# Two feed-forward stages of a fused model: the three widths of the elastic one are added before a transposed down-projection in column strips, and each group's up-projection is issued ahead of the last group's down-projection

## The chip, the cores and the metric

One core of a Trainium2 chip. The time is the device time of one execution of the whole program, in microseconds (us); several runs are taken and the median is compared.

## What is computed

The reference is a small vision and text model: patch embedding, three attention layers and two feed-forward layers (FFN), on 16 samples of 144 slots (141 tokens and 3 of padding), so 2304 rows of 192 channels, all in float32. The change touches the two FFNs alone.

```python
def _mlp_branch(xp, w1, b1, w2, b2, keep_ch):
    C = xp.shape[-1]
    cmask = (jnp.arange(C) < keep_ch).astype(xp.dtype)
    h = jax.nn.gelu(xp * cmask @ w1 + b1, approximate=False)
    return (h @ w2 + b2) * cmask
...
# L0 FFN: first half of the batch wide, second half elastic
m_large = _mlp_branch(nl2, w_fc1, b_fc1, w_fc2, b_fc2, C)
m_small = sum((gumbel_weights[i] * _mlp_branch(ns2, w_fc1, b_fc1, w_fc2, b_fc2, C // ALPHA[i]) for i in range(3)))
...
# L1 FFN
h = jax.nn.gelu(jnp.einsum('td,hd->th', xt, in_weight) + in_bias, approximate=False)
out = jnp.einsum('th,ho->to', h, out_weight)
```

`ALPHA` is 1, 2, 3, so the elastic half of the L0 FFN evaluates widths of 192, 96 and 64 channels: each width needs its own gelu of 768 hidden units, and its own part of the down-projection reaches only the first 192, 96 or 64 output channels.

## The kernel before, in words

The 2304 rows are 18 tiles of 128 (`TILES`), and an FFN works in groups of 3 tiles (`GT_` = 384 columns of the transposed activations `XT`). The 768 hidden units are 6 blocks of 128 (`HM`), counted by `m`. `feed_forward` (L1198) is called three times: "wide" for groups 0 to 2 and "elastic" for groups 3 to 5 of the L0 FFN, "last" for the 6 groups of the L1 FFN. Each call is one block in which every engine has its own program, and engines meet by semaphores.

TensorE, per group: the up-projection of all six `m` into PSUM banks 0 to 5 (L1214), then a wait for the gelus of this very group (`s_gl`), then the down-projection of the three tiles (L1247) into banks 6 and 7 by turns. In the up-projection, 192 input channels are 128 and 64: the matmul of 128 rows fills the array, and two of 64 rows stand in its upper and lower half (`tile_position` (0, 0) and (64, 0)).
In the down-projection the hidden activations are the weights of the array (128 x 128) and the rows of `w2` move: 6 `m` for each tile, and in the elastic call 6 times three, with 192, 96 and 64 moving columns and three copies of `w2` (`m_w2a`, `m_w2b`, `m_w2c`) that GpSimd has scaled by the three gumbel weights ahead of the stage (`scale_mlp`, L1185). All three widths add up in one PSUM bank.

ScalarE evaluates the gelus (L1260), VectorE adds the PSUM bank, the saved `XN`, the bias row and `H` in three steps (`finish_m`, L1287), or in one step in the last FFN (`finish_l`, L1739). ScalarE and VectorE run loops over the groups. The buffer `hid` of the gelus is single: the gelus of the next group start only when TensorE issues its up-projection, which is behind the down-projection of the group before. The last FFN stores its output group by group.

Ahead of the L0 FFN, and behind both, stand stages that are not changed: `residual_norm` with its transposes (L492 to L501), and after the L0 FFN products of expert weights (L1319) beside the next norm.

Of the kernel before, what the change touches and what calls it, by code (L numbers as in the profile page):

```python
# [20 lines left out]
ALU = mybir.AluOpType  # L21
ACT = mybir.ActivationFunctionType
AX = mybir.AxisListType

P = 128
C = 192
# [31 lines left out]
def ds(a, n):  # L58
    return bass.ds(a, n)

def fusion_kernel(nc: bass.Bass, d: dict, out: bass.AP):
    with ExitStack() as ctx:
# [3 lines left out]
        def sem(name):  # L67
            return ctx.enter_context(nc.semaphore(name))
# [1077 lines left out]
        def lsb(stack, name, shape):  # L1146
            return stack.enter_context(nc.sbuf_tensor(name, shape, F32))
# [14 lines left out]
        m_w2a, m_w2b, m_w2c = (lsb(mlp, f"m_w2{x}", [P, HM, n]) for x, n in (("a", C), ("b", 96), ("c", 64)))  # L1162
        s_wm = sem("elastic_mlp_weights")

        def load_up(sp, dst, w, s):

# [18 lines left out]
        def scale_mlp(pool):  # L1185

            pool.wait_ge(w_ffn, UP_W + 16)
            for k, (w, n) in enumerate(((m_w2a, C), (m_w2b, 96), (m_w2c, 64))):
                nc.gpsimd.tensor_scalar(w[:, :, :], m_w2[:, :, 0:n], vecs[:, V_GUM + k:V_GUM + k + 1], None, ALU.mult
                                        ).then_inc(s_wm, 1)  # L1190

        residual_norm(XN, add_to_xn, False, False, (V_N2L, V_N2S), {"sync": load_late, "gpsimd_after": scale_mlp},
                      twin=True)

        GT_ = 3 * P

        def feed_forward(tag, w1, w2s, hid, ready, b1, groups, k_rows, finish, store=None):  # L1198

            nv = len(k_rows)
            units = nv * HM
            g0, g1 = groups
            (s_up, s_gl, s_dn, s_fn, s_x, s_store) = phase_sem([
                f"{tag}_hidden", f"{tag}_gelu", f"{tag}_down", f"{tag}_finished", f"{tag}_partial", f"{tag}_stored"])
            with nc.Block() as block:  # L1206
                @block.tensor
                def _(pe):
                    for s_w, n_w in ready:
                        pe.wait_ge(s_w, n_w)  # L1210
                    def up(g, u, m, c, lo, n, first, last):

                        cols = slice((g + g0) * GT_, (g + g0 + 1) * GT_)
                        return nc.tensor.matmul(bank[u % 6][:, 0:GT_], w1[lo:lo + n, c, m * P:(m + 1) * P],  # L1214
                                                XT[lo:lo + n, c, cols], start=first, stop=last, tile_position=(lo, 0))

                    def up_pair(g, m):

                        for x in range(2):
                            pe.wait_ge(s_gl, g * units + m + x + 1)  # L1220
                            up(g, m + x, m + x, 0, 0, P, True, False)
                        for x in range(2):
                            up(g, m + x, m + x, 1, x * C1, C1, False, True).then_inc(s_up, 1)

                    def up_variants(g, m):

                        u = m * nv
                        pe.wait_ge(s_gl, g * units + u + nv)
                        up(g, u, m, 0, 0, P, True, False)
                        up(g, u + 1, m, 0, 0, k_rows[1], True, True).then_inc(s_up, 1)  # L1230
                        up(g, u, m, 1, C1, C1, False, True).then_inc(s_up, 1)
                        up(g, u + 2, m, 0, 0, k_rows[2], True, True).then_inc(s_up, 1)

                    for g in range(g1 - g0):
                        if nv == 1:
# [5 lines left out]
                        pe.wait_ge(s_gl, (g + 1) * units + 6)  # L1241
                        for j in range(3):
                            pe.wait_ge(s_fn, g * 3 + (1 if j < 2 else 2))
                            for m in range(HM):
                                for v, w in enumerate(w2s):
                                    n = w.shape[2]
                                    mm = nc.tensor.matmul(bank[6 + j % 2][:, 0:n], hid[:, m * nv + v, j * P:(j + 1) * P],  # L1247
                                                          w[:, m, :], start=(m == 0 and v == 0),
                                                          stop=(m == HM - 1), skip_group_check=True)
                            mm.then_inc(s_dn, 1)  # L1250

                @block.scalar
                def _(act):
                    act.sem_inc(s_gl, 6)  # L1254
                    with act.Fori(0, g1 - g0) as g:  # L1255
                        for m in range(HM):
                            for x, v in enumerate((0,) if nv == 1 else (1, 0, 2)):
                                u = m * nv + v
                                act.wait_ge(s_up, g * units + m * nv + x + 1)
                                nc.scalar.activation(hid[:, u, :], bank[u % 6][:, 0:GT_], ACT.Gelu,  # L1260
                                                     bias=vecs[:, b1 + m:b1 + m + 1]).then_inc(s_gl, 1)

                @block.vector
                def _(dve):
                    dve.sem_inc(s_fn, 1)
                    with dve.Fori(0, g1 - g0) as g:
                        for j in range(3):
                            dve.wait_ge(s_dn, g * 3 + j + 1)
                            finish(dve, (g + g0) * 3 + j, g * 3 + j, bank[6 + j % 2][:, 0:C], s_x, s_fn)

                if store:
                    @block.sync
                    def _(sp):
                        with sp.Fori(0, g1 - g0) as g:
                            sp.wait_ge(s_fn, g * 3 + 4)
                            sp.dma_start(out.rearrange("(t p) n -> p t n", p=P)[:, ds((g + g0) * 3, 3), :],
                                         H[:, ds((g + g0) * 3, 3), :]).then_inc(s_store, 16)
                        sp.wait_ge(s_store, 16 * (g1 - g0))

        with ExitStack() as ph:  # L1280
            def psb(name, shape, dt=F32):
                return ph.enter_context(nc.sbuf_tensor(name, shape, dt))

            hid = psb("m_hid", [P, 3 * HM, GT_])
            part = psb("m_part", [P, C])

            def finish_m(row):  # L1287
                def finish(dve, tile, count, psum, s_x, s_fn):

                    h = H[:, ds(tile, 1), :].rearrange("p t n -> p (t n)")  # L1290
                    x = XN[:, ds(tile, 1), :].rearrange("p t n -> p (t n)")
                    nc.vector.tensor_tensor(part[:, :], psum, x, ALU.add).then_inc(s_x, 1)  # L1292
                    dve.wait_ge(s_x, count * 3 + 1)
                    nc.vector.tensor_tensor(part[:, :], part[:, :], rows[:, row, :], ALU.add).then_inc(s_x, 1)
                    dve.wait_ge(s_x, count * 3 + 2)
                    nc.vector.tensor_tensor(h, part[:, :], h, ALU.add).then_inc(s_x, 1)
                    dve.wait_ge(s_x, count * 3 + 3)
                    dve.sem_inc(s_fn, 1)
                return finish

            feed_forward("wide", m_w1, (m_w2,), hid, ((w_ffn, UP_W + 16),), V_B1, (0, 3), (C,), finish_m(B2L))
            feed_forward("elastic", m_w1, (m_w2a, m_w2b, m_w2c), hid, ((s_wm, 3),), V_B1, (3, 6), (C, 96, 64),
                         finish_m(B2S))

        end_phase()
        mlp.close()
# [426 lines left out]
        with ExitStack() as ph:  # L1733
            def psb(name, shape, dt=F32):
                return ph.enter_context(nc.sbuf_tensor(name, shape, dt))

            hid = psb("l_hid", [P, HM, GT_])

            def finish_l(dve, tile, count, psum, s_x, s_fn):  # L1739
                h = H[:, ds(tile, 1), :].rearrange("p t n -> p (t n)")  # L1740
                nc.vector.tensor_tensor(h, psum, h, ALU.add).then_inc(s_fn, 1)  # L1741

            feed_forward("last", g_w1, (g_w2,), hid, ((w_last, UP_W + 16),), V_FB, (0, 6), (C,), finish_l, store=True)
        end_phase()

# [93 lines left out]
```

## Time and profile before

| | us |
|---|---|
| median of 3 runs | 1338.97 |
| the three runs | 1335.55, 1338.97, 1340.47 |
| the profiled execution | 1340.07 |
| its span in the trace | 1338.3 |
| TensorE busy | 1199.4 |
| VectorE / ScalarE / GpSimd busy | 711.5 / 769.5 / 349.3 |
| L0 FFN, first matmul to last write of `H` | 448.5 to 584.6 |
| L1 FFN, first matmul to the end of the trace | 1247.3 to 1338.3 |

A count of matmuls in a row is a count of passes, and the busy time of a group of matmuls is the time in which any of them runs, so that of passes which overlap it is smaller than their number times the mean.

### The profile page before, as it was taken

The numbers are of one execution on the slowest core, as the hardware profiler recorded it, in microseconds if no ns is written. First come the engines' busy times: TensorE is split into PE (matmuls) and PEld (weight loads), VectorE is DVE, ScalarE is ACT, GpSimd is POOL, SyncE is SP. The second block draws the span as 40 slices with busy tenths as digits, with TensorE's granted clock in tenths as the row PEclk, the third lists the DMA queues.
The fourth block names the chain that finished last, engine by engine and source line by source line (L and its number), as shares of the span: only waits on it lengthen the run. The fifth ranks groups of instructions, "written<-read, shape, count | busy, mean of one in ns | idle before, by whom it ended". The sixth has DMA issues, their size and how long they took to land. (4 is left out here: it accounts for less than half of the span.)

```text
span 1338.3 us, 34162 instructions
## 1 busy us (share of the span) xinstructions
PE 1199.4 (90%) x13220; PEld 972.4 (73%) x13220; DVE 711.5 (53%) x2290; ACT 769.5 (57%) x3346; POOL 349.3 (26%) x477
## 2 busy tenths in 40 slices
PE   6789976999997789996899999999999999995898
PEld 5479944777774456653788888988888888983465
DVE  7344465666666110023666667666666667666100
ACT  2155525677773533302877777777777777773432
POOL 2100023333332000002334433444334433441000
PEclk9789966999996799976999999999999999996799
DMA  7000000000006200001000000000000000000000
GB/s 234 20 1 1 2 1 1 1 2 2 2 2 140 44 1 1 0 1 41 2 2 2 3 2 2 2 3 2 2 2 2 2 2 3 2 2 1 9 19 27
DMA packets 34734, 19.85 MB, mean 15 GB/s; under 512 B 24592, under 2 KB 32016, under 8 KB 34576
## 3 DMA queue, kind: packets, MB, share of 16 engines
q1 hardware_dynamic: 34432, 17.20, 4.8%
q8 instruction: 106, 1.74, 0.5%
q10 hardware_dynamic: 144, 0.49, 0.1%
q14 instruction: 52, 0.43, 0.1%
HBM read 15.12 MB, written 1.77 MB: 13 GB/s over the span
## 5 line engine op out<-in xcount | busy, mean ns | idle before, releaser
L1692 POOL TENSOR_TENSOR e_W<-e_W,e_RS 128x384 f32<-128x384 f32 x256 | 203.8, 827 | 349.6 <-DVE e_RS L1620 349.6
L1563 ACT ACTIVATE e_W<-banks,e_MX 128x128 f32<-128x128 f32 x768 | 268.9, 389 | 18.3 <-DVE e_MX L1608 18.2
L1563 ACT ACTIVATION_READ_ACCUMULATOR e_W<-banks,e_MX 128x1 f32 x768 | 176.1, 229 | 0.0
L1557 ACT COPY e_PT<-banks 128x512 f32<-128x512 f32 x128 | 69.0, 588 | 105.0 <-PE banks L1468 105.0
L1420 PE MATMUL banks<-XT,e_wqk 128*128 128x141 f32 x768 | 112.2, 297 | 11.9 <-DVE e_GU L1662 8.4
L469 POOL TENSOR_TENSOR rstd<-veps,nhalf 128x6 f32<-128x6 f32 x15 | 20.6, 1373 | 365.8 <-DVE veps L435 365.8
L1420 PEld LDWEIGHTS banks<-XT,e_wqk 128*128 128x128 f32 x768 | 98.5, 194 | 14.3 <-issue 11.6
L1468 PE MATMUL banks<-ident,e_W 128*128 128x128 f32 x768 | 105.5, 273 | 2.7 <-POOL e_W L1692 1.6
L1432 PE MATMUL banks<-e_wv,XT 128*128 128x192 f32 (+1 forms) x512 | 100.2, 339 | 0.3 <-ACT e_K L1552 0.2
L1468 PEld LDWEIGHTS banks<-ident,e_W 128*128 128x128 f32 x768 | 90.3, 141 | 6.2 <-POOL e_W L1692 1.9
L1608 DVE TENSOR_REDUCE e_MX<-banks 128x3 f32<-128x384 f32 x128 | 65.4, 553 | 42.8 <-PE banks L1456 42.8
L1117 POOL TENSOR_TENSOR f_W<-f_W,f_RS 128x423 f32<-128x423 f32 x64 | 56.3, 892 | 118.8 <-DVE f_RST L1101 110.9
L1260 ACT ACTIVATE m_hid<-banks,vecs 128x384 f32<-128x384 f32 x72 | 38.8, 577 | 77.7 <-PE banks L1214 77.7
L1432 PEld LDWEIGHTS banks<-e_wv,XT 128*128 128x128 f32 (+1 forms) x512 | 75.7, 168 | 6.1 <-ACT e_K L1552 0.6
L1484 PE MATMUL banks<-e_PT,e_V 128*32 128x128 f32 x1536 | 68.7, 277 | 9.9 <-DVE e_PTT L1628 9.9
L1214 PE MATMUL banks<-XT,m_w 128*128 128x384 f32 (+1 forms) x216 | 65.7, 538 | 8.0 <-ACTq L1254 8.0
L989 ACT ACTIVATE f_W<-banks,f_MX 128x141 f32<-128x141 f32 x192 | 70.2, 394 | 2.0 <-DVE f_MX L1036 1.4
L1292 DVE TENSOR_TENSOR m_part<-banks,XN 128x192 f32<-128x192 f32 x18 | 6.4, 358 | 120.6 <-PE banks L1247 120.6
L1620 DVE RECIPROCAL e_RS<-e_SM 128x3 f32<-128x3 f32 (+1 forms) x192 | 33.9, 176 | 63.6 <-ACT e_W L1563 63.4
L1484 PEld LDWEIGHTS banks<-e_PT,e_V 128*32 128x32 f32 x1536 | 51.6, 109 | 21.1 <-DVE e_PTT L1628 16.7
L1456 PE MATMUL banks<-e_K,e_Q 32*128 32x128 f32 x1536 | 63.2, 288 | 0.0
L880 PE MATMUL banks<-ident,f_W 128*70 128x128 f32 (+1 forms) x384 | 52.5, 277 | 9.3 <-DVE f_PT L1057 7.8
(245 smaller groups left out, 2743.2 us busy)
## 6 DMA issues: line engine op xcount, KB each, us to landing
xp<-in_patches_dram SPq DMA_DIRECT2D x4, 768.0 KB, 8.2
H<-in_h_dram SPq DMA_DIRECT2D x1, 1728.0 KB, 10.3
out_dram<-H SPq DMA_DIRECT2D x6, 288.0 KB, 2.3
e_g<-in_e_gu_dram SPq DMA_DIRECT2D x1, 1536.0 KB, 8.3
e_o<-in_e_o_dram SPq DMA_DIRECT2D x4, 192.0 KB, 5.9
e_wqk<-in_e_qk_dram SPq DMA_DIRECT2D x8, 96.0 KB, 2.6
e_wqk<-in_e_qk_dram SPq DMA_DIRECT2D x24, 32.0 KB, 2.3
e_wv<-in_e_v_dram SPq DMA_DIRECT2D x4, 192.0 KB, 2.6
```

What stands on the lines that cost most here:

```text
L989: ex = nc.scalar.activation(W[n % 2][:, t, :], bank[i][:, x * SEQ:(x + 1) * SEQ], ACT.Exp, bias=MX[:, t:t + 1], accum_out=SM[n % 2][:, t:t ...
L1117: nc.gpsimd.tensor_tensor(x, x, RS[n % 2][:, 3 * i:3 * i + 3].unsqueeze(2).broadcast_to([P, 3, SEQ]), ALU.mult).then_inc(s_nm, 1)
L1214: return nc.tensor.matmul(bank[u % 6][:, 0:GT_], w1[lo:lo + n, c, m * P:(m + 1) * P], XT[lo:lo + n, c, cols], start=first, stop=last, tile ...
L1420: mm = nc.tensor.matmul(bank[6][:, m * SEQ:(m + 1) * SEQ], w[:, c, m * P:(m + 1) * P], XT[:, c, t0:t0 + SEQ], start=(m == 0 and c == 0), s ...
L1432: mm = nc.tensor.matmul(bank[6][0:nk, i * C:(i + 1) * C], XT[:, c, t0 + k0:t0 + k0 + nk], w[:, c, :], start=(i == 0 and c == 0), stop=(c = ...
L1456: mm = nc.tensor.matmul(bank[i][:, x * P:(x + 1) * P], QE[n % 2][HP * i:HP * (i + 1), q, :], KM[n % 2][HP * i:HP * (i + 1), k, 0:P], start ...
L1468: tr = nc.tensor.transpose(dst[:, (t % 4) * P:(t % 4 + 1) * P], W[n % 2][:, t, :], ident[:, :])
L1484: nc.tensor.matmul(bank[5][HP * c:HP * (c + 1), col:col + P], VP[n % 2][:, 0, h, :], PT[:, slot_of[h], :], start=(c not in seen), stop=(h ...
L1557: nc.scalar.copy(PT[:, 4 * u:4 * u + 4, :], bank[4 + u][:, 0:4 * P]).then_inc(s_pa, 1)
L1563: ex = nc.scalar.activation(W[n % 2][:, t, :], bank[i][:, x * P:(x + 1) * P], ACT.Exp, bias=MX[:, t:t + 1], accum_out=SM[n % 2][:, t:t + 1])
L1608: nc.vector.tensor_reduce(MX[:, 3 * i:3 * i + 3], bank[i][:, 0:S0].rearrange("p (x k) -> p x k", x=3), AX.X, ALU.max, negate=True).then_in ...
L1692: nc.gpsimd.tensor_tensor(x, x, RS[n % 2][:, 3 * i:3 * i + 3].unsqueeze(2).broadcast_to([P, 3, P]), ALU.mult).then_inc(s_nm, 1)
```

## The change

Both FFNs: `hid` becomes two buffers by turns; the loops of ScalarE and VectorE are written out; TensorE issues `up(0)`, then for each group `up(g + 1)` ahead of `down(g)`, so that the down-projection waits for gelus that were fed a whole up-projection earlier. ScalarE's gelus of group g wait for the down-projection of group g - 2.

The L0 FFN becomes one block for all six groups, in code of its own:

- GpSimd adds the bias row and `XN` to `H` for all 18 tiles (two steps each), then scales each gelu of the full width (`h0`) by the first gumbel weight, 18 times.
- VectorE then merges the widths of one `m`: h1 = h1 * g1 + h0, and h2 = h2 * g2 + h1. Output channels 0 to 63 need h2, 64 to 95 need h1, and 96 to 191 need h0.
- TensorE's `elastic_down` turns the roles round: `w2` is the weight and the merged gelus move, 384 columns at a time. For each `m` three matmuls write three strips of output channels, 64, 32 and 32 array columns wide (L1361), and for each second `m` two matmuls of 64 array columns write channels 128 to 191, one for either `m`, side by side (L1366). The three scaled copies of `w2` go.
- The result is transposed (channels by tokens), so ScalarE and VectorE copy it to SBUF (`DT`), and `turn_back` transposes it on TensorE: for each tile one transpose and one matmul with two stacked identities (`m_ii`), which also adds the two halves of L1366. VectorE adds the two banks to `H`, 384 and 192 columns.
- `turn_back(3)` stands in `up(5)` behind its second `m`; `turn_back(4)` and `turn_back(5)` stand at the end.

```diff
@@ L0 FFN: TensorE @@
+                    def elastic_down(g):
+                        pe.wait_ge(s_fn, 3 * min(g, G - 2))
+                        if g == G - 1:
+                            pe.wait_ge(s_gl, first[G])
+                        t0, t1 = turned(g)
+                        for m in range(HM):
+                            k = (g - WIDE) * HM + m + 1
+                            pe.wait_ge(s_h2, k)
+                            for v, lo, n in ((2, 0, 64), (1, 64, 32), (0, 96, 32)):
+                                nc.tensor.matmul(t0[lo:lo + n, 0:GT_], m_w2[:, m, lo:lo + n], hid[g % 2][:, 3 * m + v, :],
+                                                 start=(m == 0), stop=(m == HM - 1), tile_position=(0, lo),
+                                                 skip_group_check=True)
+                            if m % 2:
+                                for x in range(2):
+                                    mm = nc.tensor.matmul(t1[x * C1:(x + 1) * C1, 0:GT_], m_w2[:, m - 1 + x, P:C],
+                                                          hid[g % 2][:, 3 * (m - 1 + x), :], start=(m == 1),
+                                                          stop=(m == HM - 1), tile_position=(0, x * C1),
+                                                          skip_group_check=True)
+                        mm.then_inc(s_de, 1)
+
+                    def turn_back(g):
+                        pe.wait_ge(s_da, g - WIDE + 1)
+                        pe.wait_ge(s_dv, g - WIDE + 1)
+                        for j in range(3):
+                            dst, at = turned(g)[j // 2], j % 2 * C
+                            nc.tensor.transpose(dst[:, at:at + P], DT[g % 2][:, 0, j * P:(j + 1) * P], ident[:, :])
+                            mm = nc.tensor.matmul(dst[:, at + P:at + C], DT[g % 2][:, 1, j * P:(j + 1) * P], m_ii[:, :],
+                                                  start=True, stop=True, skip_group_check=True)
+                        mm.then_inc(s_bk, 1)
+
+                    pe.wait_ge(w_ffn, UP_W + 16)
+                    pe.wait_ge(s_ii, 1)
+                    up(0)
+                    for g in range(G):
+                        if g + 1 < G:
+                            up(g + 1)
+                        if g < WIDE:
+                            wide_down(g)
+                        else:
+                            elastic_down(g)
+                    turn_back(G - 2)
+                    turn_back(G - 1)
@@ L0 FFN: VectorE @@
+                    def merge(g):
+                        for m in range(HM):
+                            k = (g - WIDE) * HM + m + 1
+                            h0, h1, h2 = (hid[g % 2][:, 3 * m + v, :] for v in range(3))
+                            dve.wait_ge(s_h0, k)
+                            nc.vector.scalar_tensor_tensor(h1, h1, vecs[:, V_GUM + 1:V_GUM + 2], h0, ALU.mult, ALU.add
+                                                           ).then_inc(s_h1, 1)
+                            dve.wait_ge(s_h1, k)
+                            dve.wait_ge(s_gl, first[g] + 3 * m + 3)
+                            nc.vector.scalar_tensor_tensor(h2, h2, vecs[:, V_GUM + 2:V_GUM + 3], h1, ALU.mult, ALU.add
+                                                           ).then_inc(s_h2, 1)
...
+                    for g in range(WIDE, G):
+                        if g + 1 < G:
+                            merge(g + 1)
+                        finish_elastic(g)
@@ L0 FFN: GpSimd @@
+                    for t in range(TILES):
+                        nc.gpsimd.tensor_tensor(XN[:, t, :], XN[:, t, :], rows[:, B2L if t < HALF else B2S, :], ALU.add
+                                                ).then_inc(s_pre, 1)
+                        pool.wait_ge(s_pre, t + 1)
+                        nc.gpsimd.tensor_tensor(H[:, t, :], H[:, t, :], XN[:, t, :], ALU.add).then_inc(s_hx, 1)
+                    for g in range(WIDE, G):
+                        for m in range(HM):
+                            pool.wait_ge(s_gl, first[g] + 3 * m + 2)
+                            h0 = hid[g % 2][:, 3 * m, :]
+                            nc.gpsimd.tensor_scalar(h0, h0, vecs[:, V_GUM:V_GUM + 1], None, ALU.mult).then_inc(s_h0, 1)
```

TensorE from the wide groups into the elastic ones, before: an up-projection of 12 matmuls (two `m` in 4), the down-projection behind it, the seam between the two calls, and then the three widths for each `m` and tile.

```order
L1214 MATMUL banks<-XT,m_w1 128x384 x12
L1247 MATMUL banks<-m_w2,m_hid 128x192 x18
L1206 UNCONDITIONAL_BRANCH
L1207 UNCONDITIONAL_BRANCH
L1214 MATMUL banks<-XT,m_w1 128x384 x24
L1247 MATMUL banks<-m_w2a,m_hid 128x192
L1247 MATMUL banks<-m_w2b,m_hid 128x96
L1247 MATMUL banks<-m_w2c,m_hid 128x64
```

The same place after (`m_hid0` and `m_hid1` are the two buffers; L1309 is the up-projection, L1348 the wide down-projection, L1361 the strips of 64 and 2 x 32 array columns, L1366 the two of 64).

```order
L1309 MATMUL banks<-XT,m_w1 128x384 x24
L1348 MATMUL banks<-m_w2,m_hid0 128x192 x18
L1309 MATMUL banks<-XT,m_w1 128x384 x24
L1361 MATMUL banks<-m_hid1,m_w2 64x384
L1361 MATMUL banks<-m_hid1,m_w2 32x384 x2
L1361 MATMUL banks<-m_hid1,m_w2 64x384
L1361 MATMUL banks<-m_hid1,m_w2 32x384 x2
L1366 MATMUL banks<-m_hid1,m_w2 64x384 x2
```

The down-projection of group 3 now stands behind the up-projection of group 4, and 54 matmuls of a group have become 24.

VectorE at the end of the L0 FFN, before: the last three additions of the last tile, the loop's end and the next stage's first statistics.

```order
L1292 TENSOR_TENSOR m_part<-banks,XN 128x192
L1293 ISA
L1294 TENSOR_TENSOR m_part<-m_part,rows 128x192
L1295 REGISTER_ALU
L1296 REGISTER_ALU
L1296 TENSOR_TENSOR H<-m_part,H 128x192
L1297 REGISTER_ALU
```

The same place after: the last merge of group 5, then for group 4 and for group 5 the copy of the turned result and the two additions to `H`.

```order
L1438 SCALAR_TENSOR_TENSOR m_hid1<-m_hid1,vecs 128x384
L1443 COPY m_DT0<-banks 128x384
L1448 TENSOR_TENSOR H<-banks,H 128x384
L1448 TENSOR_TENSOR H<-banks,H 128x192
L1443 COPY m_DT1<-banks 128x384
L1448 TENSOR_TENSOR H<-banks,H 128x384
L1448 TENSOR_TENSOR H<-banks,H 128x192
```

The copy of group 5 (`m_DT1`) stands on VectorE behind the additions of group 4, and these wait for `turn_back(4)`, which TensorE issues behind the down-projection of group 5.

## Rows read from the trace of the kernel before

**Rows 1.** The page: the span, busy time of the engines, granted clock in 40 slices.

```profile
span 1338.3 us, 34162 instructions
PE 1199.4 (90%) x13220; PEld 972.4 (73%) x13220; DVE 711.5 (53%) x2290; ACT 769.5 (57%) x3346; POOL 349.3 (26%) x477
PEclk9789966999996799976999999999999999996799
```

**Rows 2.** Busy time by stretch, in us: cold start, an elastic down, an elastic up.

```profile
core 0: us, PE busy (x) PEld busy (x) DVE busy (x) ACT busy (x) POOL busy (x), PEclk, DMA share, GB/s
448.40:452.00 3.60, 3.48 (x6) 1.69 (x8) 0.00 (x0) 1.28 (x1) 0.00 (x0) 0.50 0.07 24
...
511.00:525.00 14.00, 14.00 (x109) 14.00 (x110) 2.15 (x6) 0.00 (x0) 0.00 (x0) 1.00 0.00 1
525.00:540.00 15.00, 13.87 (x49) 5.67 (x48) 1.07 (x3) 9.78 (x18) 0.00 (x0) 1.00 0.00 1
```

**Rows 3.** Timeline of the L0 FFN: start, length, idle before it and its releaser.

```profile
473.35 6.12 PE L1247 MATMUL banks<-m_w,m_hid 128*128 128x192 f32 x36 [1.14 <-ACT m_hid L1260]
...
495.64 4.71 PE L1214 MATMUL banks<-XT,m_w 128*128 128x384 f32 x16 [2.12 <-ACTq L1254]
...
510.83 0.59 PE L1247 MATMUL banks<-m_w2a,m_hid 128*128 128x192 f32 x2 [1.14 <-ACT m_hid L1260]
...
524.77 14.03 PE L1214 MATMUL banks<-XT,m_w 128*128 128x384 f32 x48
```

**Rows 4.** Groups of matmuls in the two FFNs: busy us, mean ns, idle before.

```profile
L1247 PE MATMUL banks<-l_w,l_hid 128*128 128x192 f32 x216 | 36.7, 329 | 6.8 <-ACT l_hid L1260 6.8
L1247 PE MATMUL banks<-m_w2a,m_hid 128*128 128x192 f32 x108 | 29.5, 355 | 3.4 <-ACT m_hid L1260 3.4
L1247 PE MATMUL banks<-m_w,m_hid 128*128 128x192 f32 x108 | 18.4, 329 | 3.4 <-ACT m_hid L1260 3.4
```

**Rows 5.** Groups with 128 moving columns: whole array (L1468) and four strips (L1484).

```profile
L1468 PE MATMUL banks<-ident,e_W 128*128 128x128 f32 x768 | 105.5, 273 | 2.7 <-POOL e_W L1692 1.6 <-DVE e_ON L1645 0.9
L1484 PE MATMUL banks<-e_PT,e_V 128*32 128x128 f32 x1536 | 68.7, 277 | 9.9 <-DVE e_PTT L1628 9.9
```

**Rows 6.** Timeline of TensorE: eight passes, four of each shape (L916), and six of one.

```profile
249.08 1.29 PE L916 MATMUL banks<-f_ON,f_wp 128*128 128x141 f32 x8
...
702.71 0.88 PE L1508 MATMUL banks<-e_ON,e_guw 128*128 128x141 f32 x6
```

**Rows 7.** Groups nearest to the added work, on VectorE, GpSimd and TensorE.

```profile
L1650 DVE COPY e_GU<-banks 128x423 f32<-128x423 f32 x16 | 9.6, 600 | 9.7 <-PE banks L1508 9.7
L786 DVE SCALAR_TENSOR_TENSOR a_WW<-a_ES,a_sr,a_TT 71x141 f32<-71x141 f32 x32 | 10.2, 359 | 0.6
L1705 POOL TENSOR_TENSOR e_WT<-e_WT,e_RST 104x152 f32<-104x152 f32 x64 | 28.3, 443 | 0.0
L1247 PE MATMUL banks<-m_w2c,m_hid 128*128 128x64 f32 x108 | 19.4, 262 | 0.0
```

**Rows 8.** Timeline: the scaling of the smallest copy, and the end of the stage.

```profile
436.45 1.31 POOL L1189 TENSOR_SCALAR m_w2c<-m_w,vecs 128x384 f32<-128x384 f32 x1
...
582.78 0.36 PE L1247 MATMUL banks<-m_w2c,m_hid 128*128 128x64 f32 x2
...
584.28 0.36 DVE L1296 TENSOR_TENSOR H<-m_part,H 128x192 f32 x1
585.71 14.96 PE L1319 MATMUL banks<-e_g,e_o 128*128 128x384 f32 x21 [2.57 <-PEq L117]
587.68 0.48 ACT L1328 COPY e_guw<-banks 128x384 f32<-128x384 f32 x1 [18.70 <-PE banks L1319]
```

**Rows 9.** Busy time by stretch behind the stage.

```profile
585.60:588.00 2.40, 2.29 (x5) 0.88 (x6) 2.26 (x14) 0.32 (x1) 0.00 (x0) 0.81 0.00 0
588.00:601.00 13.00, 13.00 (x18) 3.14 (x16) 3.27 (x17) 2.06 (x5) 2.73 (x2) 0.50 0.00 1
```

More of the change, by code:

```diff
@@ L1183, in load_late, with stack_identity, feed_forward @@
                 sp.dma_start(ew[e][1][:, :, :], d["e_v"][e]).then_inc(w_exp, 16)
[L1185 to L1192, printed above, removed]
+        def stack_identity(pool):
+            nc.gpsimd.tensor_tensor(m_ii[:, :], ident[:, 0:C1], ident[:, C1:P], ALU.add).then_inc(s_ii, 1)
+        residual_norm(XN, add_to_xn, False, False, (V_N2L, V_N2S), {"sync": load_late, "gpsimd_after": stack_identity},
                       twin=True)
         GT_ = 3 * P
[L1198 to L1203, printed above, removed]
+        def feed_forward(tag, w1, w2s, hid, ready, b1, kinds, k_rows, finish, store=None):
+            G = len(kinds)
+            first = [HM * sum(kinds[:g]) for g in range(G + 1)]
             (s_up, s_gl, s_dn, s_fn, s_x, s_store) = phase_sem([
@@ L1225, in up_variants @@
                     def up_variants(g, m):
[L1227 to L1235, printed above, removed]
+                        u = 3 * m
@@ L1244, in _ @@
                             for m in range(HM):
[L1245 to L1249, printed above, removed]
-                            mm.then_inc(s_dn, 1)
+                                for v, w in enumerate(w2s[kinds[g]]):
+                                    mm = nc.tensor.matmul(bank[6 + t % 2][:, 0:w.shape[2]],
+                                                          hid[g % 2][:, m * kinds[g] + v, j * P:(j + 1) * P], w[:, m, :],
+                                                          start=(m == 0 and v == 0), stop=(m == HM - 1),
+                                                          skip_group_check=True)
@@ L1264, in _ @@
                 def _(dve):
[L1265 to L1269, printed above, removed]
+                    for t in range(3 * G):
+                        dve.wait_ge(s_dn, t + 1)
+                        finish(dve, t, bank[6 + t % 2][:, 0:C], s_x, s_fn)
                 if store:
@@ L1273, in _ @@
                     def _(sp):
[L1274 to L1278, printed above, removed]
+                        for g in range(G):
+                            sp.wait_ge(s_fn, 3 * g + 3)
+                            sp.dma_start(out.rearrange("(t p) n -> p t n", p=P)[:, 3 * g:3 * g + 3, :],
+                                         H[:, 3 * g:3 * g + 3, :]).then_inc(s_store, 16)
+                        sp.wait_ge(s_store, 16 * G)
         with ExitStack() as ph:
@@ L1282, in psb @@
                 return ph.enter_context(nc.sbuf_tensor(name, shape, dt))
[L1284 to L1299, printed above, removed]
@@ L1301, in fusion_kernel @@
-            feed_forward("wide", m_w1, (m_w2,), hid, ((w_ffn, UP_W + 16),), V_B1, (0, 3), (C,), finish_m(B2L))
-            feed_forward("elastic", m_w1, (m_w2a, m_w2b, m_w2c), hid, ((s_wm, 3),), V_B1, (3, 6), (C, 96, 64),
-                         finish_m(B2S))
+            hid = [psb(f"m_hid{i}", [P, 3 * HM, GT_]) for i in range(2)]
+            DT = [psb(f"m_DT{i}", [P, 2, GT_]) for i in range(2)]
+            WIDE, G = 3, 6
+            first = [HM * (g + 2 * max(0, g - WIDE)) for g in range(G + 1)]
```

157 lines of the change are left out of this document (134 added, 23 removed).

## The prediction

> **What bounds the kernel now.** The page comes first [rows 1]: TensorE is busy for 1199 of 1338 us, the other engines for 26 to 57%. So a change counts where TensorE waits, or where its own work gets shorter. The stretches come next [rows 2]. In the elastic up-projection the reader sees ScalarE busy for 9.8 of 15 us, VectorE and GpSimd almost idle; in the down-projection TensorE is full for 14 of 14 us at clock 1.00 and ScalarE stands still. Up and down take turns and nothing of one covers the other. The timeline [rows 3] shows what that costs: between the last up pass and the first down pass TensorE idles 1.14 us, released by the last gelu. It does so in all 12 groups: 3.4 and 3.4 us in the L0 FFN and 6.8 us in the last FFN [rows 4]. The seam between the calls "wide" and "elastic" is 2.12 us more [rows 3].
>
> Two durations carry the sum. A pass of 192 columns costs 0.165 us: 36 take 6.12 us, the last of which lasts 0.33 [rows 3, 4]. So a pass of 384 columns is taken as 0.33. One elastic down-projection of before lasts from 510.83 to 524.77, 13.94 us for 108 passes [rows 3].
>
> **The waits that go.** `down(g)` comes behind `up(g + 1)`, at least 7 us later than the gelus that it needs. All 12 waits go, the last group's too, since `down(4)` lies between: 6.8 us in the L0 FFN, 6.8 in the last [rows 4]. What is late next? ScalarE needs 9.8 us of each 14 of the up stage [rows 2] and may run on under the down-projection, so it stays ahead. The seam goes: 2.1 us. The cold start at clock 0.50 stays as it is [rows 2].
>
> **Work that is hidden.** GpSimd adds 36 times 192 columns, at about 0.5 us (152 columns take 0.44 [rows 7]), some 18 us from 448.5 on; the first down-projection ends its first tile near 467, and GpSimd has done that tile in its first microsecond. Then it scales 18 gelus at 1.31 us, the price of the 384-column scaling of before [rows 8]. VectorE's two merges of one `m` are not in the trace: 141 columns of that operation cost 0.36 us, and so do 192 columns of an addition in SBUF [rows 7, 8]; scaled by columns 384 cost at most 0.98, and about 0.6 if a part of the 0.36 is fixed. For one `m` that is 1.31 on GpSimd and 1.2 (at most 2.0) on VectorE, against an up step of 14.03 / 6 = 2.34 us [rows 3]. Hidden, and behind the up stage lies another down-projection of 7 us or more. If that cover were gone, each group would pay the last merge, some 2.5 us. One place is tight: the finish of the last wide group is queued on VectorE behind `merge(3)`; its third tile may be late. I take 0.5 us for this and other hand-overs.
>
> **The down-projection turned round.** This is where the choice lies. A group has 24 matmuls of two passes instead of 54. The trace shows strips of the array side by side: 1536 passes of 128 columns in four strips keep TensorE busy for 68.7 us, 0.045 each, while 768 passes of the same 128 columns on the whole array take 105.5, 0.137 each [rows 5]. But those four strips have one width. Here one of 64 and two of 32 array columns follow each other. The trace has no pair of unlike shapes that could run side by side, so it shows only what a change of shape costs where they could not: four passes of 128 and four of 64 array columns take 1.29 us, six of one shape 0.88, which makes 1.12 for eight at 0.12; a change costs 0.17 at most [rows 6]. In the up step, four full passes (1.32) and a pair in two halves (0.66) make 1.98, and it takes 2.34: 0.36 for a change in and one out and what the halves lack [rows 3]. I take 0.15 for a change, with 0 and 0.2 as ends.
>
> If a change of shape lets the array finish first, the 64-strip runs alone, the two of 32 together, and the two of 64 (L1366) together: 6 + 6 + 3 = 15 stretches of two passes, 15 x 0.66 = 9.9 us, and 13 changes 2.0, together 11.9 us (9.9 to 12.5). If only the place in the array counts, the three strips run together: 9 x 0.66 = 5.9 and 0.9 for the pairs, 6.8 us. I take the first, since every group that runs side by side in the trace has one shape, and each change of shape that it does show has its price.
>
> The Trainium skill bears on this. The page "TensorEngine Tiling (Array Packing)", section Key Properties, says that "Changing tiling mode (not just tile) drains the TensorE", and its list of modes holds 128x64 and 128x32 as two of them. By it the strips of 64 and 32 cannot overlap and the down-projection is 11.9 us; without it, 6.8. The price of a change in the rows agrees with a drain, but no row here shows two unlike strips that were kept apart.
>
> So the sum takes 13.94 - 11.9 = 2.04 us for a group, 6.1 us for three.
>
> **What is added on the path.** `turn_back` is three transposes of one pass (0.14 or less [rows 5]) and six short passes (about 0.1; the 108 passes of the old down-projection have a mean of 0.13, and these are its shortest kind [rows 3, 7]): 1.0 us, 1.1 with a change. `turn_back(3)` stands in `up(5)`: its copies (0.48 on ScalarE [rows 8], about 0.55 on VectorE [rows 7]) lie under two up steps, so it costs its 1.1 us.
> The end is longer than it looks. Before, the last pass ends at 582.78 + 0.36 = 583.14 and `H` is complete at 584.64: 1.5 us [rows 8]. After, VectorE copies group 5's half only behind group 4's additions, which wait for `turn_back(4)`: 1.1 (turn back) + 0.25 (hand-over) + 1.0 (additions of 384 and 192 columns, 0.55 + 0.36) + 0.55 (copy) + 0.1 + 1.1 + 0.25 + 1.0 = 5.4 us, 3.9 more.
> Behind the stage TensorE runs at clock 0.81 for 2.4 us and then at 0.50 [rows 9]. After five sparse microseconds the half clock should come earlier: 5 passes in 2.3 us would take up to 1.4 more. I take 1.0.
>
> **The sum.** 6.8 + 2.1 + 6.1 - 0.5 - 1.1 - 3.9 - 1.0 = 8.5 in and behind the L0 FFN, and 6.8 in the last: 15.3 us. The profiled execution took 1340.07 (span 1338.3 and 1.8 around it), which becomes 1324.8; the median of the runs is 1.1 lower, so 1323.7.
>
> **The rivals.**
> Unlike strips overlap: the down-projection is 6.8 us, the gain in it 3 x 7.1 = 21.4, the sum 30.6, the time 1308.4. For it speaks how freely the four strips run [rows 5]; against it the price of each change [rows 6]. By the page's rule it cannot be. Chance 0.34.
> The change doesn't do what it says: strips of 384 columns do not overlap at all, 24 x 0.66 + 2.0 = 17.8 us, 3.9 longer than before in each group; what is left of the sum is 9.2 - 11.6 = -2.4, the time 1341.4, no difference that can be told. Against it speak rows 5. Chance 0.06.
> Slower: every strip matmul waits until its forerunner has left the array, as the pair of halves seems to, 0.66 + 0.36 = 1.02 us each [rows 3]. Then 24 cost 24.5 us, 31.7 more in three groups, the time is 1361.5. It ends above +0.5% from 0.80 us for a strip matmul on (a down-projection of 19.2). Against it speak again rows 5. Chance 0.03.
> The granted clock falls in the elastic stage, for which nothing speaks (1.00 in up and down alike [rows 2], and 0.9 where strips run in the experts' stage [rows 1]): each microsecond of work at half clock costs one more. Chance 0.03, half of it slower.
>
> **How the numbers follow.** The forecast has 0.54. Its own range is 1317 to 1329: 9.9 or 12.5 us for the down-projection is -6 or +2, and tail, waits and clock are good for 3 either way. The whole range reaches down to the overlap, 1305 to 1330; some 0.05 is below it and 0.14 above. A measurement of this kernel tells about 0.5% from no change (1332.3 to 1345.7): faster 0.54 + 0.34 = 0.88, same 0.07, slower 0.05.
>
> **What would show each step.** In the trace after: no idle before the down matmuls of either FFN, and the last FFN shorter by 6 to 7.5 us. The stretch from an elastic up to the next is 11.9 us (6.8 if unlike strips overlap, above 15 if nothing does), and starts of the 64-strip and the 32-strips 0.7 us apart, or a few nanoseconds. GpSimd's 1.31 us stays below 2.3 beside VectorE. From the last strip matmul to the last write of `H` 5 to 6 us, with VectorE's second copy behind two additions. The prediction is wrong if the starts of unlike strips coincide, or if a merge ends later than the down-projection that waits for it.

## The result, and the profile of the kernel after

| us | before | after |
|---|---|---|
| median (4 runs each) | 1337.26 | 1316.21 |
| lowest and highest | 1334.41, 1340.47 | 1315.01, 1316.62 |
| profiled execution, its span | 1340.07, 1338.3 | 1316.51, 1314.8 |
| L0 FFN, first matmul to last write of `H` | 136.1 | 122.5 |
| from there to the experts' first matmul | 42.35 | 42.69 |
| experts' stage, up to the last FFN | 620.4 | 619.0 |
| last FFN, first matmul to last write of `H` | 87.6 | 80.3 |

The ratio of the medians is 0.984, 95% interval 0.9814 to 0.9867: 21 us faster, where 15.3 were forecast. Two further measurements of the same kernel gave 0.9853 (0.9833 to 0.9872) and 0.9841 (0.9823 to 0.9859); the medians of the three are 21.1, 19.4 and 22.1 us below those of before. The last four rows of the table come from one trace of each kernel.

The page of after, for [rows 1]:

```profile
span 1314.8 us, 33568 instructions
PE 1190.5 (91%) x13067; PEld 939.6 (71%) x13067; DVE 718.5 (55%) x2290; ACT 762.4 (58%) x3342; POOL 390.1 (30%) x529
PEclk8779976999997699966999999999999999996699
```

TensorE's busy time falls by 9 us only, the span by 23.5: most of what went was idle time. The timeline of TensorE, for [rows 3] (start, length, operation, idle before it in brackets); L1309 is the up-projection, L1348 the wide down-projection:

```profile
476.11 6.12 PE L1348 MATMUL banks<-m_w,m_hid 128*128 128x192 f32 x36
482.06 13.97 PE L1309 MATMUL banks<-XT,m_w 128*128 128x384 f32 x48
495.97 6.27 PE L1348 MATMUL banks<-m_w,m_hid 128*128 128x192 f32 x36
...
515.99 3.19 PE L1361 MATMUL banks<-m_hid,m_w 128*64 128x384 f32 x12
519.10 0.87 PE L1366 MATMUL banks<-m_hid,m_w 128*64 128x384 f32 x4
519.80 3.14 PE L1361 MATMUL banks<-m_hid,m_w 128*64 128x384 f32 x12
...
527.42 4.74 PE L1309 MATMUL banks<-XT,m_w 128*128 128x384 f32 x16
532.10 0.33 PE L1377 MATMUL banks<-ident,m_DT 128*128 128x128 f32 x1
...
533.00 9.36 PE L1309 MATMUL banks<-XT,m_w 128*128 128x384 f32 x32
```

No row has a bracket, so TensorE does not idle in front of any of them: neither the 1.14 us before each down-projection nor the seam of 2.12 is left. An elastic down-projection now reaches from 515.99 to 527.42, 11.43 us (13.94 before). Two `m` of it take 3.76 (519.80 to 523.56, where the next row of L1361 starts). Its passes by shape, from 516.0 to 527.3:

```profile
L1361 PE MATMUL banks<-m_hid,m_w 128*64 128x384 f32 x12 | 5.1, 503 | 0.0
L1361 PE MATMUL banks<-m_hid,m_w 128*32 128x384 f32 x24 | 5.0, 498 | 0.0
L1366 PE MATMUL banks<-m_hid,m_w 128*64 128x384 f32 x12 | 2.6, 512 | 0.0
```

The 24 passes in strips of 32 stand two side by side and take no longer than the 12 of the single strip of 64. The three rows add up to 12.7 us in a stretch of 11.3: unlike strips hardly share time.

Groups of after, for [rows 4, 7, 8] (busy us, mean ns of one, idle before and its releaser):

```profile
L1361 PE MATMUL banks<-m_hid,m_w 128*32 128x384 f32 (+1 forms) x108 | 28.3, 499 | 0.0
L1471 POOL TENSOR_SCALAR m_hid<-m_hid,vecs 128x384 f32<-128x384 f32 x18 | 26.2, 1458 | 49.5 <-ACT m_hid L1407 49.5
L1438 DVE SCALAR_TENSOR_TENSOR m_hid<-m_hid,vecs 128x384 f32<-128x384 f32 x18 | 11.1, 619 | 0.6
L1463 POOL TENSOR_TENSOR XN<-XN,rows 128x192 f32<-128x192 f32 x18 | 10.6, 590 | 17.9 <-SPq L1304 17.9
...
L1247 PE MATMUL banks<-l_w,l_hid 128*128 128x192 f32 x216 | 36.4, 328 | 0.0
```

The last row is the last FFN: 0.0 idle for 6.8. The end of the L0 FFN, TensorE and then VectorE:

```profile
564.22 0.87 PE L1366 MATMUL banks<-m_hid,m_w 128*64 128x384 f32 x4
565.01 0.33 PE L1377 MATMUL banks<-ident,m_DT 128*128 128x128 f32 x1
...
567.65 0.30 PE L1377 MATMUL banks<-ident,m_DT 128*128 128x128 f32 x1 [1.57 <-DVE m_DT L1443]
```

```profile
566.22 0.82 DVE L1448 TENSOR_TENSOR H<-banks,H 128x384 f32<-128x384 f32 x2 [11.82 <-PE banks L1378]
566.96 0.55 DVE L1443 COPY m_DT<-banks 128x384 f32<-128x384 f32 x1
568.83 0.82 DVE L1448 TENSOR_TENSOR H<-banks,H 128x384 f32<-128x384 f32 x2 [1.33 <-PE banks L1378]
```

From the last strip pass (565.09) to the last write of `H` (569.65) it is 4.56 us. TensorE idles 1.57 for VectorE's copy of group 5, which stands behind group 4's additions.

Busy time by stretch behind the stage, for [rows 9]:

```profile
core 0: us, PE busy (x) PEld busy (x) DVE busy (x) ACT busy (x) POOL busy (x), PEclk, DMA share, GB/s
565.00:571.00 6.00, 2.67 (x22) 2.17 (x20) 2.65 (x8) 0.48 (x1) 0.00 (x0) 1.00 0.00 0
571.00:573.00 2.00, 2.00 (x5) 0.57 (x4) 1.97 (x14) 0.00 (x0) 0.18 (x1) 0.53 0.00 0
573.00:588.00 15.00, 15.00 (x20) 3.65 (x20) 3.02 (x16) 2.38 (x5) 2.55 (x2) 0.50 0.00 0
```

From 565 to 571 TensorE is busy for 2.67 of 6 us at clock 1.00; the next products start at 570.46, and from 571 on the clock is 0.53 and then 0.50. Over the first 2.4 us of the products (570.46 to 572.86) it is 0.64, and 0.79 over the same 2.4 us before (585.70 to 588.10): the half clock comes about 0.7 us earlier.

### The profile page after: what moved, and what is told of

The parts are those of the page before. It is cut to its first block and busy times, and to the rows that moved or that the text cites. A ratio compares the mean times of both kernels' runs of the same rounds, so it can differ in the third digit from the quotient of the medians.

```text
span 1314.8 us, 33568 instructions
## 1 busy us (share of the span) xinstructions
PE 1190.5 (91%) x13067; PEld 939.6 (71%) x13067; DVE 718.5 (55%) x2290; ACT 762.4 (58%) x3342; POOL 390.1 (30%) x529
## 3 DMA queue, kind: packets, MB, share of 16 engines
HBM read 15.12 MB, written 1.77 MB: 13 GB/s over the span
## 5 line engine op out<-in xcount | busy, mean ns | idle before, releaser
L1309 PE MATMUL banks<-XT,m_w 128*128 128x384 f32 (+1 forms) x216 | 65.2, 536 | 7.3 <-PEq L117 7.3
L1780 DVE TENSOR_REDUCE e_MX<-banks 128x6 f32<-128x768 f32 x64 | 60.6, 947 | 0.0
```

The source lines that it names most:

```text
L1309: return nc.tensor.matmul(bank[u % 6][:, 0:GT_], m_w1[lo:lo + n, c, m * P:(m + 1) * P], XT[lo:lo + n, c, g * GT_:(g + 1) * GT_], start=sta ...
L1780: nc.vector.tensor_reduce(MX[:, 6:12].rearrange("p (i x) -> p i x", i=2), pair23[:, :, 0:S0].rearrange("p i (x k) -> p i x k", x=3), AX.X, ...
```

## The experiments

The theory of the next three: strips of 64 and of 32 array columns are two shapes, and the array finishes one before the other starts; this, not their place, makes the down-projection 11.4 us. The rival: strips of 384 columns don't overlap freely in any shape, or the price lies in something else (weights, merges). All kernels but three_widths_kept are the changed one with the edit shown. "After" stands for the changed kernel.

**One shape for a step (strips32_t0).** The strip of 64 is written as two of 32:

```diff
-                            for v, lo, n in ((2, 0, 64), (1, 64, 32), (0, 96, 32)):
+                            for v, lo, n in ((2, 0, 32), (2, 32, 32), (1, 64, 32), (0, 96, 32)):
```

> The 64-column strip of each m is split into two matmuls of 32 array columns, so that the four strips of L1361 have one shape; the pairs of L1366 stay at 64. Theory (a change of shape lets the array finish first): the four strips start within nanoseconds of each other and the elastic down-projection falls from 11.43 us to 3 x (2 x 0.645 + 0.645 + 2 x 0.12) + 0.1 = 6.6 us, 14.5 us less in three groups, time about 1301.7. Rival (it is the third moving stream that the array cannot take beside the other two, whatever the shape): the 32-column strips of h2 run apart from those of h1 and h0 and the down-projection stays at 11 us or more, time 1316 or above.

```profile
520.36 1.50 PE L1361 MATMUL banks<-m_hid,m_w 128*32 128x384 f32 x16
521.79 0.87 PE L1366 MATMUL banks<-m_hid,m_w 128*64 128x384 f32 x4
522.58 1.50 PE L1361 MATMUL banks<-m_hid,m_w 128*32 128x384 f32 x16
```

The timeline shows the four strips of an `m` running side by side: more matmuls (16 passes for 12, two `m`) take 1.43 us where they took 3.1. The down-projection lasts from 520.36 to 527.03, 6.67 us. The median is 1302.42, ratio 0.9732 (0.9716 to 0.9748). The theory's numbers, 6.6 and 1301.7, are met. The strips of h2, h1 and h0 now run together, so it is not the third moving stream that kept them apart.

**One shape throughout (strips32_all).** The edit above, and the pairs of L1366 become four strips of 32 too:

```diff
+                                    for lo in (0, 32):
+                                        mm = nc.tensor.matmul(t1[x * C1 + lo:x * C1 + lo + 32, 0:GT_],
+                                                              m_w2[:, m - 1 + x, P + lo:P + lo + 32],
```

> As strips32_t0, and the two 64-column matmuls of L1366 are four of 32 as well, so that the elastic down-projection has one shape throughout. Theory: 9 stretches of two passes and no change between, 9 x 0.645 + 0.1 = 5.9 us instead of 11.43, 16.6 us less in three groups, time about 1299.6, and 0.7 us per group less than strips32_t0. Rival (third stream): no gain, and about 11 us.

```profile
512.75 1.50 PE L1361 MATMUL banks<-m_hid,m_w 128*32 128x384 f32 x16
514.06 0.83 PE L1367 MATMUL banks<-m_hid,m_w 128*32 128x384 f32 x8
514.71 1.47 PE L1361 MATMUL banks<-m_hid,m_w 128*32 128x384 f32 x16
...
518.69 4.74 PE L1309 MATMUL banks<-XT,m_w 128*128 128x384 f32 x16
```

512.75 to 518.69 is 5.94 us: nine rounds of four strips, each with two passes, and one change at the end. The five changes that strips32_t0 has more cost (6.67 - 5.94) / 5 = 0.146 us each. The median is 1296.65, ratio 0.9706 (0.9672 to 0.974), where 1299.6 was expected; the L0 FFN lasts 106.2 us, 16.3 less than after, and 3 x 5.49 = 16.5 had to go. (The median gained 3 more. In this trace the stage starts at 443.8, in that of after at 447.1; over all traces of the changed kernel and its variants the start lies between 443.8 and 451.0, so that part is scatter and not the edit's.)

**The same strips, fewer changes (by_shape, by_shape_again).** All matmuls of 64 array columns of a group first, then the 12 of 32; nothing is split:

```diff
                         for m in range(HM):
+                            pe.wait_ge(s_h2, (g - WIDE) * HM + m + 1)
+                            strip(m, 2, 0, 64)
...
+                        for m in range(HM):
+                            strip(m, 1, 64, 32)
+                            mm = strip(m, 0, 96, 32)
```

> The same matmuls as in the changed kernel, in another order: in each elastic down-projection all 64-column ones first (h2 of each m, and the pairs), then the 32-column pairs of all m. Nothing more runs side by side than before; only the 13 changes of shape become 3. Theory: 15 stretches of 0.645 and 0.3 = 10.0 us instead of 11.43, 4.4 us less in three groups, time about 1311.8; a change is worth 0.12 us. Rival (the 0.41 us at a change is the wait for another moving tensor, not for the shape): between h1/h0 and h2 nothing is gained, the stretches stay at 0.76 us, 11.4 us, time 1316.

```profile
521.49 1.07 PE L1366 MATMUL banks<-m_hid,m_w 128*64 128x384 f32 x3
522.50 4.06 PE L1358 MATMUL banks<-m_hid,m_w 128*32 128x384 f32 x24
526.49 3.89 PE L1309 MATMUL banks<-XT,m_w 128*128 128x384 f32 x12
```

The rows are those of the second measurement. In both traces the down-projection lasts 9.94 us (516.55 to 526.49 in the second): 1.49 less for 11 changes less, 0.135 each. Yet the first median, 1316.54, ratio 0.9842 (0.9826 to 0.9859), was no lower than that of after, and the 4.5 us that the expectation had were missing. So both were measured again, together on one chip.

> The changed kernel once more, in the same company as the next two, to tell differences of 4 us. Medians of the two earlier runs of it were 1316.2 and 1320.7. Both theories: 1316 to 1321; elastic down-projection 11.4 us.

> The reordering by shape once more, beside the changed kernel on the same chip: the 64-column matmuls first, then the pairs of 32. If a change of shape costs what the trace shows (three down-projections of 9.94 instead of 11.43 us), it is 4.5 us below after_third, a ratio of the two of 0.9966. If that gain is lost elsewhere, as the equal medians of the first comparison would have it, the two are within 1.5 us.

After had 1317.37, ratio 0.9841 (0.9823 to 0.9859), by_shape 1313.05, ratio 0.9807 (0.9794 to 0.9819): 4.3 us apart, with intervals that do not meet. The gain is there. It was there in the trace of the first measurement too: the L0 FFN lasted 118.5 us in it for 122.5 in after, and that execution took 1312.15. The other three, of 1316 to 1318, have no trace, so where they lost the gain is not shown.

**The order alone (three_widths_kept).** The pipelined order, the two buffers, the one block and the changed last FFN are kept; the elastic down-projection is the old one with three scaled copies of `w2`, 54 matmuls a group, and merges and `turn_back` are left out.

> One part of the change alone: one block for all six groups of the L0 FFN, two hid buffers, the next group's up-projection first, and the last FFN as in the change; but the elastic down-projection of before with its three scaled copies of w2, and the three additions on VectorE. Theory: against the changed kernel each of three down-projections takes 13.94 instead of 11.43 us (7.5 more), turn_back(3) goes (0.95 less) and the tail is 1.5 instead of 4.6 us (3.1 less): 3.5 us more than the changed kernel in the L0 FFN, whose span becomes 126 us, time about 1319.7. Rival (the pipelined order alone is not worth the 16.9 us of waits and seam, so that the turned down-projection gave most): a span of 130 us or more, time above 1323.

```profile
501.99 13.97 PE L1210 MATMUL banks<-XT,m_w 128*128 128x384 f32 x48
515.89 0.59 PE L1251 MATMUL banks<-m_w2a,m_hid 128*128 128x192 f32 x2
...
529.83 14.03 PE L1210 MATMUL banks<-XT,m_w 128*128 128x384 f32 x48
```

515.89 to 529.83 is the old 13.94 us. The L0 FFN lasts 125.2 us, 10.9 less than before; the last FFN 79.2. The median is 1322.34, ratio 0.988 (0.986 to 0.9899), where 1319.7 was expected; and after on the same chip:

> The changed kernel once more, as the yardstick on the same chip for the three others: 1316.2 as before, with the elastic down-projection at 11.43 us; what differs between two executions in stages that no edit touches shows how much of a difference of medians is none of the edit's.

It had 1320.74, ratio 0.9853 (0.9833 to 0.9872), also 4 us above its first median. So 17.8 of the 19.4 us that after gains here come from the order. The turned down-projection, as it is written, brings 1.6 us of the median, and the two intervals meet, so that the medians alone do not show it. The traces do: the L0 FFN lasts 125.2 us with the old down-projection and 123.3, 122.5 and 121.7 in the three traces of after, 2 to 3.5 less. By the parts, the three groups win 7.7 and the tail (1.2 for 4.6) and `turn_back(3)` take 4.3 back.

**The last FFN in turn (last_in_turn).** In the last FFN alone, TensorE takes up- and down-projection by turns again:

```diff
-                    up(0)
                     for g in range(G):
-                        if g + 1 < G:
-                            up(g + 1)
+                        up(g)
                         down(g)
```

> Only the last FFN: up(g) and down(g) in turn again on TensorE (no next group's up-projection ahead), with everything else of the change kept, the two hid buffers and the written-out loops too. Theory: the wait for the gelus comes back, 1.21 us in each of 6 groups, 7.3 us more, time about 1323.5. Rival (the written-out loops or the missing table loads gave the gain, not the order): time stays at 1316 to 1318.

```profile
L1247 PE MATMUL banks<-l_w,l_hid 128*128 128x192 f32 x216 | 36.7, 329 | 6.8 <-ACT l_hid L1268 6.8
```

All 6.8 us are back in the group's row, the last FFN lasts 86.7 us (79.2 to 80.3 in the traces of after), the median is 1324.34, ratio 0.99 (0.9879 to 0.992). The buffers and the written-out loops, which stay, do not give the gain without the order.

**The tail (one_shape_tail).** strips32_all, and `turn_back(4)` stands in the last down-projection behind `m` = 1:

```diff
+                            if m == 1 and g == G - 1:
+                                turn_back(G - 2)
...
-                    turn_back(G - 2)
                     turn_back(G - 1)
```

> strips32_all, and turn_back(4) is issued inside the down-projection of group 5, behind its second m, so that VectorE's additions of group 4 and the copy of group 5 no longer follow one another at the end. Theory (the tail of 4.6 us is a chain of turn back, additions, copy, turn back, additions): 0.95 + 0.25 + 0.82 less, the tail from the last strip pass to the last write of H becomes 2.6 us, time 1.9 us less than strips32_all, about 1294.7. Rival (the end is set by the next stage's start, not by this chain): no difference to strips32_all.

```profile
548.37 0.33 PE L1381 MATMUL banks<-ident,m_DT 128*128 128x128 f32 x1
...
552.62 0.83 PE L1367 MATMUL banks<-m_hid,m_w 128*32 128x384 f32 x8
554.22 0.30 PE L1381 MATMUL banks<-ident,m_DT 128*128 128x128 f32 x1 [0.77 <-DVE m_DT L1446]
```

The tail shrinks from 4.57 to 2.77 us and TensorE's wait in it from 1.57 to 0.77. But the 1.0 us of `turn_back(4)` (548.37 to 549.37) is now inside the down-projection, so only the 0.8 of the wait is won: L0 FFN 105.7 for 106.2. The expectation counted the moved work as gone. It missed: the median is 1300.40 for 1294.7, ratio 0.9703 (0.9685 to 0.9721), which can't be told from that of strips32_all.

**The full passes of an up-projection together (one_shape_up_six, _again, _third).** On top of one_shape_tail, the same rule of one shape in the wide groups and the last FFN: the six matmuls of 128 rows first, then the three pairs of halves:

```diff
-                        for x in range(2):
+                        for x in range(HM):
...
-                            up_part(g, m + x, m + x, 1, x * C1, C1, False, True).then_inc(s_up, 1)
+                            up_part(g, m + x, m + x, 1, x % 2 * C1, C1, False, True).then_inc(s_up, 1)
```

> one_shape_tail, and in the wide up-projections and those of the last FFN all twelve full passes of six m come first, then the three pairs of 64 rows: one change of shape in and one out for a group instead of three. Theory (each change costs about 0.1 us and the first pass behind it 0.1 more, also with strips of rows): a step of 2.335 x 3 = 7.0 us becomes 12 x 0.3225 + 6 x 0.3225 + 0.3 = 6.1 us, 0.9 in each of 9 groups, 8 us less than one_shape_tail, about 1287. Rival (ScalarE, which now gets its first gelu later, holds up the banks of the next up-projection): 0 to 3 us less, with waits before the up-projection.

> All column strips of 32, the one turn_back inside the last down-projection, and the full passes of an up-projection ahead of its three half pairs. Its four runs were 1281.4, 1281.7, 1293.6 and 1297.1. If its work is 33 us shorter than that of after (3 x 5.5 in the elastic down-projections, 9 x 0.8 in the wide up-projections, 0.8 in the tail and the cold starts) the fast end is about 24.5 us and with cheaper cold starts 28 below after_third: 1288 to 1294. If runs of 1281 return, they show a higher granted clock in the whole (0.935 against 0.918), and the difference lies in stages that no edit touches.

The last FFN of the second measurement, an up-projection and its neighbours:

```profile
1230.01 6.12 PE L1247 MATMUL banks<-l_w,l_hid 128*128 128x192 f32 x36
1235.96 6.17 PE L1206 MATMUL banks<-XT,l_w 128*128 128x384 f32 x24
1242.06 6.12 PE L1247 MATMUL banks<-l_w,l_hid 128*128 128x192 f32 x36
```

1235.96 to 1242.06 is 6.10 us for 6.90: 0.8 less for a group, by four changes fewer, where 0.9 was expected; nine groups have it. The last FFN lasts 74.7 us. The medians are 1287.64 (0.9599, 0.9551 to 0.9647) and 1292.17 (0.9622, 0.9582 to 0.9662). It beats both kernels, but its runs have two levels: 1280.5 to 1281.7, and 1288.9 to 1297.1. A median of such a mixture says little about the edit. Its traced work does: against one_shape_tail the L0 FFN lost 1.9 us (105.7 to 103.8) and the last FFN 4.3 (79.2 to 74.8), 6.2 where 8 were forecast. A third trace met the lower level.

> A third look at the best version, for its two levels of time (1280 to 1282, and 1289 to 1297). If this execution is one of the short ones, its trace shows where the clock is higher: against the trace of the second look one stretch at clock 0.50 of 12 to 15 us is missing, most likely the one behind the L0 FFN (13 us of 0.50 in rows 9), or one in the cold starts. If it is one of the long ones, the question stays open.

Its median of two runs is 1286.26, ratio 0.9605 (0.9502 to 0.9709); the profiled one took 1280.52. The products behind the L0 FFN, in the second trace and then in the third:

```profile
553.70 24.32 PE L1490 MATMUL banks<-e_g,e_o 128*128 128x384 f32 x32 [1.77 <-PEq L117]
```

```profile
550.19 13.07 PE L1490 MATMUL banks<-e_g,e_o 128*128 128x384 f32 x32 [1.77 <-PEq L117]
```

And the busy time by stretch there (stretch, length, then by engine, and the granted clock), second and third trace:

```profile
553.00:566.00 13.00, 12.30 (x17) 3.29 (x18) 5.53 (x30) 1.56 (x4) 2.73 (x2) 0.53 0.00 0
```

```profile
553.00:566.00 13.00, 12.05 (x38) 4.08 (x36) 4.50 (x22) 5.44 (x19) 2.27 (x2) 1.00 0.00 0
```

The same instructions ran at 1.2 GHz almost throughout in the one and at 2.4 GHz in the other, behind the same tail with its idle of 0.77 and 1.77 us. From the end of the L0 FFN to the experts it is 31.8 us for 43.3, which is the larger part of the 14.9 us between the two spans (1278.8 and 1293.7). Of before and after no trace showed the short case, and neither has runs with such a gap. Why the clock stays up in some executions of this kernel is open.

## Why the prediction was right, point by point

- **Sign and mechanism.** Right: faster, by the case that had 0.54. The median 1316.2 lies in the range of 1305 to 1330, and 0.8 below that case's own 1317. The size was 6 us short. That case's own range, 1317 to 1329, did not hold it: its upper end has the 3 us for tail, waits and clock, but its lower end (1323.7 - 6 = 1317.7) leaves them out. With them it would have been 1314.7.
- **The waits that go.** Right, and what is next is not late: 0.0 idle. An up- and a down-projection together take 12.85 us for 14.06, 1.21 less where 1.14 was counted. The last FFN is 7.3 us shorter (8.1 and 8.4 in the two other traces of after) for 6.8, the seam 2.3 for 2.1. last_in_turn brings the 6.8 back.
- **Work that is hidden.** Right. The merge is 0.62 us as taken; GpSimd's scaling is 1.46 on average for 1.31 (1.25 with VectorE idle, up to 1.65 beside a merge), its additions 0.59 for 0.5; all are below the 2.3 us of an up step. The tight place is real but small: VectorE's addition for the last wide group starts at 499.62, right behind a merge, and `down(2)` takes 6.27 for 6.12, 0.15 us where 0.5 was kept for it. The merges are the cause: three_widths_kept has none, and there `down(2)` takes 5.95 us from its start to the next up-projection, for 6.11 in after.
The rival (1308.4) falls as an account of this kernel, but its 6.8 us is nearly what strips32_t0 has, 6.67 us, by giving the strips of an `m` one shape.
- **`turn_back` and the tail.** `turn_back(3)` takes 0.9 (532.10 to 533.00) for 1.1; the tail 4.56 (5.1 in another trace) for 5.4, in the forecast order of steps; the two additions are 0.82 for 1.0, and that twice.
- **The clock behind.** From the end of the stage to the experts it is 0.3 us longer in this trace, 1.0 in the two others, for 1.0.
- **The sum.** In the L0 FFN 13.6 us went where 9.5 were forecast (8.5 and the 1.0 that is behind it). The 4.1 between are: down-projections 1.65 (34.2 us for the three where 42.0 stood), tail 0.8, the six waits 0.55, hand-overs 0.35, `turn_back(3)` 0.2, seam 0.2, and a cold start (the first two up-projections, in part at clock 0.50) that was 0.35 shorter. Each unknown was taken on the dear side, and such margins add up: that is the step that missed. The cold start is scatter, 15.4 to 16.5 us for its 48 passes in the three traces of after. The last FFN adds 0.5 to 1.6. In this pair of traces the span fell by 23.5 us; 2.7 of them lie ahead of the stage and in the experts' stage, which the change does not touch.
- The two rivals in which strips don't overlap, and the fall of the clock in the elastic stage (1.00 in its stretches), have nothing for them in any run: TensorE's clock is 1.00 from 516.0 to 542.0 in after, over an elastic down- and up-projection.

## What to carry to other kernels

Issue the next group's up-projection ahead of this group's down-projection, and the wait for the activations goes in full if the other engine has slack; here that, with the seam between two calls gone, was worth 17.8 of 19.4 us. Where matmuls are placed side by side in the array, cut them into strips of one shape, even if that makes more of them: splitting a strip of 64 into two of 32 took the down-projection from 11.43 to 6.67 us. When work is moved out of a tail to an earlier place on the same busy engine, only the wait in the tail is won, not the work; and a gain of 4 us in 1300 needs the two kernels side by side.

## What the runs showed of the hardware

- The up-projections had changes of shape to give away as well: four fewer are worth 0.8 us a group, 0.2 each, in which stands whatever the pairs of halves win by standing together; the two are not told apart.
- Four strips of 32 array columns and 384 moving columns overlap in full: (5.94 - 0.135) / 9 = 0.645 us for the two passes of all four. One matmul on the whole array takes the same 0.645 (starts at 1235.963 and 1236.608 in the second trace of one_shape_up_six).
- GpSimd's scaling of 384 columns takes 1.25 us alone and up to 1.65 beside VectorE's merges in SBUF (after).
- The same 32 passes behind the L0 FFN took 24.3 or 13.1 us from one execution to the next of one kernel, by the granted clock alone.
